# Attention scores as two full-height products of stacked queries, with two more key transfers a batch

## The chip, the cores and the metric

The kernel runs on one core of a Trainium2 chip. The metric is the device time of one execution in microseconds, the median of three runs. A core has TensorE (PE, with its weight loads PEld), VectorE (DVE), ScalarE (ACT), GpSimd (POOL) and SyncE (SP), which here only issues transfers.

## The reference

A cross-attention block and a mixture of experts over 16 batches of 256 tokens of width 256, in float32:

```
h = layernorm(x);  q = (h @ Wq + bq) as 16 heads of 16
k, v = (ctx @ Wkv + bkv) as 16 heads of 16, 77 context rows
scores = einsum('bqhd,bkhd->bhqk', q, k) / 4
x = x + (softmax(scores) @ v) @ Wp + bp
x = x + sum over the 2 best of 8 experts of gate * expert(layernorm(layernorm(x)))
```

## The kernel before

The first 300 us or so are the attention. Its 4096 tokens are 32 row tiles of 128 tokens (NT), two for each batch b of 16. A round i works on several tiles at once: it forms the scores of tile i, transposes and multiplies the probabilities of tile i-1, projects tile i-2, makes the new residual row (`x1`) of tile i-2, and prepares the queries and values of batch nb = i // 2 + 1, which rounds 2 nb and 2 nb + 1 will use. An even round is the first of a batch. Each engine runs one program in its own written order; semaphores hold them together. After round 31 the expert tiles follow; the change leaves their instructions as they are.

**Scores.** The 16 heads are two chunks (m = 0, 1) of 128 query channels, and a chunk is two halves (g = 0, 1) of 64 channels, four heads each. The keys of four heads stand as blocks on a diagonal of `k_blocks` (4 x 77 = 308 columns), so that one product of 64 channels gives the 308 scores of four heads. For float32 accuracy query and key are each split into a high and a low float32r part, and three products are summed: high query x high key, low query x high key, high query x low key. Both halves of one chunk are written as alternating products, each on its own 64 of the 128 rows of TensorE and into its own PSUM bank (L1727 to L1743). There are three score banks in turn, u = 4 i + 2 m + g; the six products of a chunk wait once, for the bank of the second half.

**Queries.** In an odd round ACT writes `q_t` (L927) and rounds it to `q_h` (L932, one operation on 128 partitions), and DVE subtracts to `q_l` (L1279, one operation).

**Keys.** `k_parts` holds high and low keys of two batches. SP's queue spreads them over the diagonal with eight transfers a batch, one for each head of a chunk (`spread_keys`, L517), in an even round, behind the store of `x1` (L539) that waits for DVE. In the odd round it issues a load of x (L498), every second time one of the context (L503), and two loads of values (`load_values`, L531 and L534), then the next store of `x1`.

**DVE.** `softmax_input` takes the maxima of both halves (L1238) and subtracts them (L1244), which frees the score banks.

Of the kernel before, what the change touches and what calls it, by code (L numbers as in the profile page):

```python
# [8 lines left out]
F32 = mybir.dt.float32  # L9
F32R = mybir.dt.float32r  # L10
# [3 lines left out]
ACTF = mybir.ActivationFunctionType  # L14
AXX = mybir.AxisListType.X

P = 128
BATCH, SEQ, D = 16, 256, 256
CTX = 77
# [235 lines left out]
def build(nc, a, out):  # L255
    with ExitStack() as ctx:
# [8 lines left out]
        def sems(name, n):  # L265
            return [sem(f"{name}{i}") for i in range(n)]
# [7 lines left out]
        f_x, f_ctx = sems("f_x", XR), sems("f_ctx", 2)  # L274
        f_kblocks, f_vstore, f_vload = (sems(n, 2) for n in ("f_kblocks", "f_vstore", "f_vload"))
        f_x1, f_put = sems("f_x1_", 3), sems("f_put", ZR)
# [84 lines left out]
        xl[0] = sb("xl0", [P, DC, WIDTH], F32R)  # L361
        wh[0] = sb("wh0", [P, 3, 2, HIDDEN], F32R)
        wl[0] = sb("wl0", [P, 3, 2, HIDDEN], F32R)

# [8 lines left out]
        v_rep = [sb(f"v_rep{i}", [P, KB, VW]) for i in range(2)]  # L373
        k_blocks = [sb(f"k_blocks{i}", [P, 2, DC, HPB, CTX], F32R) for i in range(2)]
        q_h = [sb(f"q_h{i}", [P, DC, SEQ], F32R) for i in range(2)]
        q_l = [sb(f"q_l{i}", [P, DC, SEQ], F32R) for i in range(2)]
        v_blocks = [sb(f"v_blocks{i}", [P, KB, BLOCK_HEADS, VW]) for i in range(2)]
# [115 lines left out]
        def sync_program(e):  # L493
# [14 lines left out]
            def spread_keys(b):  # L508

                e.wait_ge(k_low, b // 2 + 1)  # L510
                if b == 0:
                    e.wait_ge(blocks_ready, 2)
                if b >= 2:
                    e.wait_ge(scores_mm, SCORES_OF_BATCH * (b - 1))
                for h in range(HPC):
                    part = slice(h * HD, (h + 1) * HD)
                    e.dma_start(k_blocks[b % 2][part, :, :, h % HPB, :].bitcast(F32),  # L517
                                k_parts[part, :, :, b % 2, :].bitcast(F32)).then_inc(
                                    f_kblocks[b % 2], 16)

            def store_values(b):
# [116 lines left out]
            for i in range(FIRST_ROUND, OVERLAP + 2):  # L638
# [11 lines left out]
                if batch and i % 2:  # L650
                    load_values(nb)
                if i == EARLY_TILES + 9:
                    load_matrix(0, 0)
                    wait_puts(EARLY_TILES // 2)
                    load_rows(0)
# [8 lines left out]
                if batch and i % 2 == 0:  # L664
                    if nb == 0:
                        spread_keys(nb)
                    store_values(nb)
                    if nb:
                        spread_keys(nb)
# [56 lines left out]
        def pool_program(e):  # L726
# [79 lines left out]
            for i in range(2):  # L806
                e.memset(k_blocks[i][:, :, :, :, :].bitcast(F32), 0.0).then_inc(blocks_ready, 1)
            e.memset(half[:, :], -0.5).then_inc(half_ready, 1)
# [83 lines left out]
        def act_program(e):  # L892
# [26 lines left out]
            def queries(b):  # L919
                ps = misc_of("q", b)  # L920
                e.wait_ge(q_mm, b + 1)
                if b:
                    e.wait_ge(q_low, b)
                else:
                    e.wait_ge(bq_ready, 1)
                for m in range(DC):
                    e.activation(q_t[:, m, :], ps[:, m * SEQ:(m + 1) * SEQ], ACTF.Identity,  # L927
                                 bias=bq_scaled[:, m:m + 1], scale=SCALE).then_inc(q_out, 1)
                e.wait_ge(q_out, 2 * b + 2)
                if b >= 2:  # L930
                    e.wait_ge(scores_mm, SCORES_OF_BATCH * (b - 1))
                e.activation(q_h[b % 2][:, :, :], q_t[:, :, :], ACTF.Copy).then_inc(q_high, 1)  # L932

# [286 lines left out]
        def dve_program(e):  # L1220
# [56 lines left out]
            def low_queries(b):  # L1277
                e.wait_ge(q_high, b + 1)
                e.tensor_tensor(q_l[b % 2][:, :, :], q_t[:, :, :],  # L1279
                                q_h[b % 2][:, :, :].bitcast(F32), ALU.subtract).then_inc(q_low, 1)  # L1280

# [436 lines left out]
        def pe_program(e):  # L1718
# [8 lines left out]
            def scores(i, m):  # L1727
                b, s = divmod(i, 2)
                if s == 0 and m == 0:
                    e.wait_ge(q_low, b + 1)  # L1730
                    e.wait_ge(f_kblocks[b % 2], 16 * HPC * (b // 2 + 1))
                u0 = 4 * i + 2 * m
                if u0 >= 2:
                    e.wait_ge(less_max, u0 - 1)
                for k, (qs, w) in enumerate(((q_h, 0), (q_l, 0), (q_h, 1))):
                    for g in range(2):
                        mm = e.matmul(  # L1737
                            score_bank[(u0 + g) % 3][:, 0:HPB * CTX],
                            qs[b % 2][g * HALF:(g + 1) * HALF, m, s * P:(s + 1) * P],
                            k_blocks[b % 2][g * HALF:(g + 1) * HALF, w, m, :, :].rearrange(  # L1740
                                "p h k -> p (h k)"), start=(k == 0), stop=(k == 2))
                        if k == 2:
                            mm.then_inc(scores_mm, 1)  # L1743

# [421 lines left out]
```

## Time and profile before

| | |
|---|---|
| median of 3 runs | 935.6 us (935.13 to 937.54) |
| the profiled execution's own time | 938.24 us |
| its span, first to last instruction | 936.4 us |
| busy share of the span: PE, PEld, DVE, ACT, POOL | 95%, 85%, 80%, 69%, 44% |
| mean granted TensorE clock | 0.989 of full speed |
| attention, about | 0 to 300 us |

The shares are means over stages with different limits, so they don't tell what a part of the attention waits for; its rows do. Times in rows are counted from the first instruction, 1.8 us of the profiled time lie outside the span.

### The profile page before, as it was taken

What the parts mean: (1) busy time and instruction counts of PE and PEld (TensorE: products, weight loads), DVE (VectorE), ACT (ScalarE), POOL (GpSimd) and SP (SyncE); (2) the same over time, 40 slices, a digit from 0 to 9 for tenths busy, and PEclk for the clock granted to TensorE, in tenths of its full rate; (3) what the DMA queues carried; (4) which work ended last, traced back from release to release, by engine and by line L of the source; (5) the groups of instructions that cost most, each with busy time, mean ns of one, the idle gap of its engine ahead of it and who ended that gap; (6) DMA issues with size and microseconds to landing.
All of it is one profiled execution on the core that took longest, in us unless ns stands there. A gap on an engine that the chain in (4) does not pass through costs nothing.

```text
span 936.4 us, 19131 instructions
## 1 busy us (share of the span) xinstructions
PE 887.6 (95%) x6174; PEld 795.6 (85%) x6174; DVE 745.0 (80%) x1757; ACT 646.3 (69%) x1297; POOL 408.9 (44%) x649
## 2 busy tenths in 40 slices
PE   4999999999998998999999999999999999999995
PEld 3888878887877876788999989899898998998994
DVE  2688888888878888787979788887877877778783
ACT  3676766767666774775977777867776776777773
POOL 3456576777776575330432240605114234052052
PEclk8899999999999999999999999999999999999998
DMA  6332333342255337643756455827817838466442
GB/s 144 66 67 49 74 85 69 86 99 61 63 128 177 114 118 268 182 112 121 217 121 185 135 155 168 240 94 186 278 45 215 282 68 259 177 178 177 147 79 27
DMA packets 132368, 129.17 MB, mean 138 GB/s; under 512 B 59936, under 2 KB 117152, under 8 KB 132128
## 3 DMA queue, kind: packets, MB, share of 16 engines
q1 hardware_dynamic: 119392, 110.36, 38.7%
q0 software_dynamic: 12864, 17.44, 10.3%
q8 instruction: 55, 0.90, 0.4%
q14 instruction: 57, 0.47, 0.2%
HBM read 102.01 MB, written 25.36 MB: 136 GB/s over the span
## 4 chain that ended last, share of the span: by engine, by line
PE 78%; DVE 11%; issue 3%; ACT 3%; another core or an unknown queue 1%; POOL 1%; SPq 1%; DMA 0%; POOLq 0%; DVEq 0%; ACTq 0%
PE bank L1985 35%; PE bank L2029 18%; PE bank L1820 5%; PE bank L1737 4%; PE bank L1977 3%; PE bank L1755 3%; PE bank L1774 2%; DVE maxes L1238 2%; PE bank L1784 2%; PE bank L2017 1%; PE bank L1954 1%; DVE probs L1244 1%; DVE q_l L1279 1%; PE bank L1792 1%
## 5 line engine op out<-in xcount | busy, mean ns | idle before, releaser
L852 POOL DMA_INDIRECT out_rows<-yo,token x68 | 114.4, 1682 | 384.9 <-ACT yo L1095 319.8
L1985 PE MATMUL bank<-xh,wh 128*128 128x512 f32 (+1 forms) x672 | 234.7, 349 | 5.4 <-DVE gate_in L1610 4.8
L1985 PE MATMUL bank<-xl,wh 128*128 128x512 f32 (+1 forms) x672 | 228.9, 341 | 0.0
L1985 PE MATMUL bank<-xh,wl 128*128 128x512 f32 (+1 forms) x672 | 228.5, 340 | 0.0
L1586 DVE TENSOR_TENSOR wl<-raw,wh 128x1024 fp32r<-128x1024 f32 x126 | 152.4, 1220 | 13.0 <-ACT wh L1026 12.1
L1985 PEld LDWEIGHTS bank<-xh,wh 128*128 128x128 f32 x672 | 127.9, 190 | 20.1 <-DVE gate_in L1610 7.5
L2029 PE MATMUL bank<-wh,hh 128*128 128x256 f32 x496 | 141.9, 286 | 1.7 <-issue 1.3
L1985 PEld LDWEIGHTS bank<-xh,wl 128*128 128x128 f32 x672 | 127.8, 190 | 14.9
L2029 PE MATMUL bank<-wh,hl 128*128 128x256 f32 x496 | 140.4, 283 | 0.0
L2029 PE MATMUL bank<-wl,hh 128*128 128x256 f32 x496 | 140.4, 283 | 0.0
L1985 PEld LDWEIGHTS bank<-xl,wh 128*128 128x128 f32 x672 | 128.2, 191 | 10.8
L1026 ACT ACTIVATE wh<-raw 128x1024 fp32r<-128x1024 f32 x126 | 131.1, 1054 | 0.0
L1630 DVE TENSOR_TENSOR hl<-gate_in,hh 128x512 fp32r<-128x512 f32 x128 | 87.9, 686 | 44.8 <-ACT hh L1089 29.7
L1089 ACT ACTIVATE hh<-gate_in 128x512 fp32r<-128x512 f32 x128 | 80.2, 626 | 31.4 <-DVE gate_in L1623 28.9
L1064 ACT ACTIVATE gate_in<-bank,par 128x512 f32<-128x512 f32 x88 | 60.2, 684 | 59.7 <-PE bank L1985 54.3
L2029 PEld LDWEIGHTS bank<-wh,hh 128*128 128x128 f32 x496 | 95.0, 192 | 5.0 <-issue 1.5
L2029 PEld LDWEIGHTS bank<-wl,hh 128*128 128x128 f32 x496 | 95.1, 192 | 2.6
L2029 PEld LDWEIGHTS bank<-wh,hl 128*128 128x128 f32 x496 | 94.9, 191 | 0.0
L1076 ACT ACTIVATE gate_in<-gate_in 128x512 f32<-128x512 f32 (+1 forms) x144 | 86.0, 598 | 0.0
L1238 DVE TENSOR_REDUCE maxes<-bank 128x4 f32<-128x308 f32 x128 | 55.1, 469 | 32.0 <-PE bank L1737 26.3
L799 POOL DMA_INDIRECT z_rows<-z,slot x64 | 69.2, 1081 | 21.2 <-issue 17.7
L1820 PE MATMUL bank<-v_blocks,probs_t 128*128 128x102 f32 (+4 forms) x640 | 76.9, 274 | 0.6 <-ACT probs_t L951 0.4
(195 smaller groups left out, 1861.6 us busy)
## 6 DMA issues: line engine op xcount, KB each, us to landing
raw<-in_W SPq DMA_DIRECT2D x42, 1024.0 KB
raw<-in_Wo SPq DMA_DIRECT2D x25, 1024.0 KB
whole<-in_W SPq DMA_DIRECT2D x8, 1024.0 KB, 7.6
xs<-in_x SPq DMA_DIRECT2D x32, 128.0 KB, 2.7
out_rows<-x SPq DMA_DIRECT2D x32, 128.0 KB, 1.8
shared<-z_rows SPq DMA_DIRECT2D x7, 520.0 KB
bo_row<-in_bo SPq DMA_DIRECT2D x25, 128.0 KB
k_blocks<-k_parts SPq DMA_DIRECT2D x128, 19.2 KB
```

The costliest lines, as they stand in the source:

```text
L799: e.indirect_dma_start(out=z_rows, out_offset=bass.IndirectOffsetOnAxis(ap=slot[:, 2 * p + t, k:k + 1], axis=0), in_=z[p % ZR][:, t, :], i ...
L852: e.indirect_dma_start(out=out, out_offset=bass.IndirectOffsetOnAxis(ap=token[j % 4][:, s:s + 1], axis=0), in_=yo[j % 2][:, s, :], in_offs ...
L1026: e.activation(wh[split_before(j) % 2][:, w, c, :], raw[w][:, c, :], ACTF.Copy).then_inc(w_high, 1)
L1064: e.activation(dst[:, :], ps[:, 0:WIDTH], ACTF.Identity, bias=par[j % PR][:, X_B2 + u:X_B2 + u + 1]).then_inc(gate_out, 1)
L1076: e.activation(gate_in[n % 3][:, 0:w], gate_in[n % 3][:, 0:w], ACTF.Silu).then_inc(silu_made, 1)
L1089: e.activation(dst, hid[n % 3][:, 0:w], ACTF.Copy).then_inc(hid_high, 1)
L1238: e.tensor_reduce(maxes[i % 2][:, hs], view, AXX, ALU.max).then_inc(max_found, 1)
L1586: e.tensor_tensor(wl[q][:, w, c, :], raw[w][:, c, :], wh[q][:, w, c, :].bitcast(F32), ALU.subtract).then_inc(w_low, 1)
L1630: e.tensor_tensor(hl[n % (HR - 1)][:, :], hid[n % 3][:, :], hh[n % HR][:, :].bitcast(F32), ALU.subtract).then_inc(hid_low, 1)
L1820: mm = e.matmul(out, probs_t[i % 2][0:size, k, :], moving, start=(k == 0), stop=(k == KB - 1), skip_group_check=True)
L1985: mm = e.matmul(ps[:, h * cols:(h + 1) * cols], ws[split_before(j) % 2][:, w, c, m * P:(m + 1) * P], xx[j % 2][:, c, 0:cols], start=(h == ...
L2029: mm = e.matmul(down_bank[s // 2][:, (s % 2) * D:(s % 2 + 1) * D], hs[:, at:at + P], ws[q][:, 2, m // 4, (m % 4) * D:(m % 4 + 1) * D], sta ...
```

## The change

- The queries of half g are stacked: `q_parts[:, m, g, :]` has the high part on the 64 partitions of that half and the low part on the other 64. ACT rounds each half by itself and DVE subtracts each half by itself, writing to the other partitions.
- `k_blocks` gets a place for each half of all 128 partitions. With w = 0 the high keys stand on their own 64 partitions and, copied, on the other 64; with w = 1 the low keys stand on their own and zeros (from a memset) on the others. One product of 128 rows with w = 0 gives high x high plus low x high; one with w = 1 gives high x low. So a half takes two products of 128 rows, and a chunk four.
- The copy is `double_keys`: SP waits until the eight transfers of the batch have landed and issues two more, each 64 partitions x 2 x 308 float32 (154 KB). For batch 0 it stands right behind them, ahead of the store of values; for the others behind `load_values` in the odd round. PE waits for them (`f_kdouble`).
- The halves follow each other on PE. The first waits for its own bank only, which was freed a chunk earlier; the second has the wait that all six had.
- The blocks of even batches lie in the memory of weights that are loaded after the attention; the memsets at the start are twice as large.

```diff
@@ sync_program
                 for h in range(HPC):
+                    g, j = divmod(h, HPB)
                     part = slice(h * HD, (h + 1) * HD)
-                    e.dma_start(k_blocks[b % 2][part, :, :, h % HPB, :].bitcast(F32),
+                    e.dma_start(k_blocks[b % 2][part, :, :, g, j, :].bitcast(F32),
...
+            def double_keys(b):
+
+                e.wait_ge(f_kblocks[b % 2], 16 * HPC * (b // 2 + 1))
+                for g in range(2):
+                    own, other = (slice(r * HALF, (r + 1) * HALF) for r in (g, 1 - g))
+                    e.dma_start(k_blocks[b % 2][other, 0, :, g, :, :].bitcast(F32),
+                                k_blocks[b % 2][own, 0, :, g, :, :].bitcast(F32)).then_inc(
+                                    f_kdouble[b % 2], 16)
...
                 if batch and i % 2:
                     load_values(nb)
+                    if nb:
+                        double_keys(nb)
...
                     if nb == 0:
                         spread_keys(nb)
+                        double_keys(nb)
                     store_values(nb)
@@ pool_program
-                e.memset(k_blocks[i][:, :, :, :, :].bitcast(F32), 0.0).then_inc(blocks_ready, 1)
+                e.memset(k_blocks[i][:, :, :, :, :, :].bitcast(F32), 0.0).then_inc(blocks_ready, 1)
@@ act_program, queries
-                e.activation(q_h[b % 2][:, :, :], q_t[:, :, :], ACTF.Copy).then_inc(q_high, 1)
+                for g in range(2):
+                    part = slice(g * HALF, (g + 1) * HALF)
+                    e.activation(q_parts[b % 2][part, :, g, :], q_t[part, :, :],
+                                 ACTF.Copy).then_inc(q_high, 1)
@@ dve_program, low_queries
-                e.wait_ge(q_high, b + 1)
-                e.tensor_tensor(q_l[b % 2][:, :, :], q_t[:, :, :],
-                                q_h[b % 2][:, :, :].bitcast(F32), ALU.subtract).then_inc(q_low, 1)
+                for g in range(2):
+                    part = slice(g * HALF, (g + 1) * HALF)
+                    other = slice((1 - g) * HALF, (2 - g) * HALF)
+                    e.wait_ge(q_high, 2 * b + g + 1)
+                    e.tensor_tensor(q_parts[b % 2][other, :, g, :], q_t[part, :, :],
+                                    q_parts[b % 2][part, :, g, :].bitcast(F32),
+                                    ALU.subtract).then_inc(q_low, 1)
@@ pe_program, scores
                 if s == 0 and m == 0:
-                    e.wait_ge(q_low, b + 1)
                     e.wait_ge(f_kblocks[b % 2], 16 * HPC * (b // 2 + 1))
+                    e.wait_ge(f_kdouble[b % 2], 32 * (b // 2 + 1))
                 u0 = 4 * i + 2 * m
-                if u0 >= 2:
-                    e.wait_ge(less_max, u0 - 1)
-                for k, (qs, w) in enumerate(((q_h, 0), (q_l, 0), (q_h, 1))):
-                    for g in range(2):
-                        mm = e.matmul(
-                            score_bank[(u0 + g) % 3][:, 0:HPB * CTX],
-                            qs[b % 2][g * HALF:(g + 1) * HALF, m, s * P:(s + 1) * P],
-                            k_blocks[b % 2][g * HALF:(g + 1) * HALF, w, m, :, :].rearrange(
-                                "p h k -> p (h k)"), start=(k == 0), stop=(k == 2))
-                        if k == 2:
-                            mm.then_inc(scores_mm, 1)
+                for g in range(2):
+                    if s == 0 and m == 0:
+                        e.wait_ge(q_low, 2 * b + g + 1)
+                    if u0 + g >= 3:
+                        e.wait_ge(less_max, u0 + g - 2)
+                    for k in range(2):
+                        mm = e.matmul(score_bank[(u0 + g) % 3][:, 0:HPB * CTX],
+                                      q_parts[b % 2][:, m, g, s * P:(s + 1) * P],
+                                      k_blocks[b % 2][:, k, m, g, :, :].rearrange(
+                                          "p h k -> p (h k)"),
+                                      start=(k == 0), stop=(k == 1))
+                    mm.then_inc(scores_mm, 1)
```

On SP's queue these rows stand around the values of batch 3, before the change:

```order
L539 DMA out_rows<-x_2 128x256
L523 DMA v_flat<-v_sb 77x16x17
L517 DMA k_blocks<-k_parts 16x4x77 x8
L498 DMA xs<-in_x 128x256
L503 DMA raw<-in_ctx 128x308
L531 DMA v_rep<-v_flat 128x9x17
L534 DMA v_rep<-v_flat 80x17
L539 DMA out_rows<-x_0 128x256
```

The same place of the changed kernel, where the numbers of lines are its own:

```order
L554 DMA out_rows<-x_2 128x256
L538 DMA v_flat<-v_sb 77x16x17
L523 DMA k_blocks<-k_parts 16x4x77 x8
L503 DMA xs<-in_x 128x256
L508 DMA raw<-in_ctx 128x308
L546 DMA v_rep<-v_flat 128x9x17
L549 DMA v_rep<-v_flat 80x17
L532 DMA k_blocks<-k_blocks 64x2x308 x2
L554 DMA out_rows<-x_0 128x256
```

Only the two copies are new; they are the last transfers ahead of the scores that need them. On PE a round's start, from the transposes of a later tile to the second chunk of scores, reads before:

```order
L1792 MATMUL bank<-const,xn 128x128 x2
L1755 MATMUL bank<-const,probs 128x128 x4
L1763 MATMUL bank<-const,attn 128x128 x2
L1755 MATMUL bank<-const,probs 128x128 x4
L1841 MATMUL bank<-raw,shared 128x154 x4
L1853 MATMUL bank<-shared,raw 77x256 x2
L1737 MATMUL bank<-k_blocks,q_h 128x308 x2
L1737 MATMUL bank<-k_blocks,q_l 128x308 x2
```

and in the changed kernel:

```order
L1818 MATMUL bank<-const,xn 128x128 x2
L1781 MATMUL bank<-const,probs 128x128 x4
L1789 MATMUL bank<-const,attn 128x128 x2
L1781 MATMUL bank<-const,probs 128x128 x4
L1867 MATMUL bank<-raw,shared 128x154 x4
L1879 MATMUL bank<-shared,raw 77x256 x2
L1764 MATMUL bank<-k_blocks,q_parts 128x308 x4
L1781 MATMUL bank<-const,probs 128x128
```

Nothing moves past anything else; four products stand where six stood.

## Rows read from the trace of the kernel before

**Rows 1.** Windows: us, then busy us (instructions) of PE, PEld, DVE, ACT, POOL, clock, DMA.

```profile
50.00:115.00 65.00, 64.39 (x492) 55.26 (x491) 53.80 (x180) 46.53 (x120) 38.40 (x81) 1.00 0.29 59
150.00:186.00 36.00, 34.18 (x262) 29.14 (x262) 29.99 (x107) 24.81 (x67) 26.24 (x49) 1.00 0.37 83
```

**Rows 2.** Waits of PE from 115 to 262 us: total, times, longest.

```profile
PE bank L1737 <- DVE probs L1244: 5.3, 6, 1.3
```

**Rows 3.** Timeline of PE, first scores of batch 8: start, us, instruction, form, count.

```profile
152.75 1.05 PE L1820 MATMUL bank<-v_blocks,probs_t 128*128 128x102 f32 x8
153.74 0.41 PE L1737 MATMUL bank<-k_blocks,q_h 64*128 64x308 f32 x2
153.99 0.30 PE L1737 MATMUL bank<-k_blocks,q_l 64*128 64x308 f32 x2
...
154.36 0.44 PE L1792 MATMUL bank<-const,xn 128*128 128x128 f32 x2
```

**Rows 4.** Timeline of PE in the experts: full-height float32r products of 256 columns.

```profile
520.00 0.28 PE L1985 MATMUL bank<-xh,wh 128*128 128x256 f32 x1
520.12 0.28 PE L1985 MATMUL bank<-xl,wh 128*128 128x256 f32 x1
```

**Rows 5.** The tile q_h: count, ns min/median/max, first and last start, form.

```profile
L932 ACT ACTIVATE q_h<-q_t x16: 629/630/631, 16.4 to 278.2; 128x512 fp32r<-128x512 f32 x16
L1279 DVE TENSOR_TENSOR q_l<-q_t,q_h x16: 654/962/1251, 17.0 to 282.2; 128x512 fp32r<-128x512 f32 x16
```

**Rows 6.** Timeline of DVE in round 15: its wait ahead of x1.

```profile
153.70 0.42 DVE L1274 TENSOR_TENSOR x<-bank,xs 128x256 f32<-128x256 f32 x1 [1.13 <-remote]
```

**Rows 7.** Timeline of SP's queue, batch 3: the last value load, the next store.

```profile
64.20 0.60 SPq L534 DMA_DIRECT2D v_rep<-v_flat  x1
64.88 0.40 SPq L539 DMA_DIRECT2D out_rows<-x  x1
```

**Rows 8.** DMA issues from 0 to 300 us: count, KB each, median us from issue to landing.

```profile
out_rows<-x SPq DMA_DIRECT2D x29, 128.0 KB, 1.8
...
raw<-in_ctx SPq DMA_DIRECT2D x8, 154.0 KB, 2.7
```

**Rows 9.** Timeline of SP's queue, the last value load of batch 2.

```profile
47.83 0.62 SPq L534 DMA_DIRECT2D v_rep<-v_flat  x1
```

**Rows 10.** Timeline of PE, first scores of batch 2.

```profile
49.81 0.41 PE L1737 MATMUL bank<-k_blocks,q_h 64*128 64x308 f32 x2
```

**Rows 11.** Timeline of PE, first scores of batch 3.

```profile
65.55 0.41 PE L1737 MATMUL bank<-k_blocks,q_h 64*128 64x308 f32 x2
```

**Rows 12.** Timeline of SP's queue, the last value load of batch 9.

```profile
170.44 0.57 SPq L534 DMA_DIRECT2D v_rep<-v_flat  x1
```

**Rows 13.** Timeline of PE, first scores of batch 9 and second chunk of that round.

```profile
171.72 0.41 PE L1737 MATMUL bank<-k_blocks,q_h 64*128 64x308 f32 x2
...
176.83 0.40 PE L1737 MATMUL bank<-k_blocks,q_h 64*128 64x308 f32 x2 [0.56 <-DVE probs L1244]
```

**Rows 14.** Timeline of SP's queue, the last value load of batch 8.

```profile
151.10 0.62 SPq L534 DMA_DIRECT2D v_rep<-v_flat  x1
```

**Rows 15.** Timeline of SP's queue at the start: keys of batch 0, then its values' store.

```profile
13.09 5.27 SPq L517 DMA_DIRECT2D k_blocks<-k_parts  x8
18.41 0.59 SPq L523 DMA_DIRECT2D v_flat<-v_sb  x1
...
31.43 0.60 SPq L534 DMA_DIRECT2D v_rep<-v_flat  x1
```

**Rows 16.** Timeline of PE at the start: first scores of batch 0 and of batch 1.

```profile
19.80 0.63 PE L1737 MATMUL bank<-k_blocks,q_h 64*128 64x308 f32 x2 [4.36 <-DMA k_blocks<-k_parts]
...
33.92 0.41 PE L1737 MATMUL bank<-k_blocks,q_h 64*128 64x308 f32 x2
```

**Rows 17.** Timeline of POOL at the start: the memsets, and a wait for values.

```profile
0.73 2.19 POOL L807 MEMSET k_blocks<- 128x1232 f32 x2 [0.29 <-POOLq L2155]
...
25.88 1.77 POOL L787 TENSOR_TENSOR v_blocks<-v_rep,const 128x153 f32<-128x153 f32 x6 [10.17 <-DMA v_rep<-v_flat]
```

More of the change, by code:

```diff
@@ L274, in build @@
         f_x, f_ctx = sems("f_x", XR), sems("f_ctx", 2)
-        f_kblocks, f_vstore, f_vload = (sems(n, 2) for n in ("f_kblocks", "f_vstore", "f_vload"))
+        f_kblocks, f_kdouble, f_vstore, f_vload = (
+            sems(n, 2) for n in ("f_kblocks", "f_kdouble", "f_vstore", "f_vload"))
         f_x1, f_put = sems("f_x1_", 3), sems("f_put", ZR)
@@ L361, in build @@
         xl[0] = sb("xl0", [P, DC, WIDTH], F32R)
-        wh[0] = sb("wh0", [P, 3, 2, HIDDEN], F32R)
-        wl[0] = sb("wl0", [P, 3, 2, HIDDEN], F32R)
+        first_parts = sb("first_parts", [P, 3, 2, 2, HIDDEN], F32R)
+        wh[0], wl[0] = first_parts[:, :, 0, :, :], first_parts[:, :, 1, :, :]
         scope.append(ExitStack())
@@ L373, in build @@
         v_rep = [sb(f"v_rep{i}", [P, KB, VW]) for i in range(2)]
-        k_blocks = [sb(f"k_blocks{i}", [P, 2, DC, HPB, CTX], F32R) for i in range(2)]
-        q_h = [sb(f"q_h{i}", [P, DC, SEQ], F32R) for i in range(2)]
-        q_l = [sb(f"q_l{i}", [P, DC, SEQ], F32R) for i in range(2)]
+        k_blocks = [first_parts[:, 2, :, :, :].rearrange("p w c n -> p (w c n)")[
+            :, 0:4 * DC * HPB * CTX].rearrange("p (w m g h k) -> p w m g h k", w=2, m=DC, g=2, h=HPB),
+                    sb("k_blocks1", [P, 2, DC, 2, HPB, CTX], F32R)]
+        q_parts = [sb(f"q_parts{i}", [P, DC, 2, SEQ], F32R) for i in range(2)]
         v_blocks = [sb(f"v_blocks{i}", [P, KB, BLOCK_HEADS, VW]) for i in range(2)]
@@ L510, in spread_keys @@
                 e.wait_ge(k_low, b // 2 + 1)
-                if b == 0:
-                    e.wait_ge(blocks_ready, 2)
+                if b < 2:
+                    e.wait_ge(blocks_ready, b + 1)
                 if b >= 2:
@@ L922, in queries @@
                 if b:
-                    e.wait_ge(q_low, b)
+                    e.wait_ge(q_low, 2 * b)
                 else:
```

## The prediction

> **What bounds the kernel now.** I read the windows first, to see which engine is full in which stretch of the attention; then PE's waits, to see where it isn't the bound; then the timelines of PE, SP's queue and DVE around the first scores of a batch, since the change adds a wait there; then the sizes and landings of transfers.
>
> In the windows [rows 1] PE is busy 64.39 of 65.00 us between 50 and 115 us: that stretch is PE's alone, and DVE has 11 us to spare. From 150 to 186 us PE has 34.18 of 36.00, so 1.8 us of idle in two batches. The waits say whose that is: from 115 to 262 us PE waits 5.3 us in 6 waits, 0.9 us each, for DVE's subtraction ahead of scores [rows 2]. So up to round 11 every us on PE counts, and later PE and DVE hand the path to each other: PE from the second chunk of an even round through the odd round's scores, then DVE, which has maxima, queries, x1 and softmax to do before the second chunk of the next even round.
>
> **What the change takes away.** *Products.* The two halves of a pair already run at once: two instructions take 0.41 us together, and the next pair starts 0.25 us behind [rows 3]. Six products fill 0.62 us (153.74 to 154.36). Ahead of them is a gap: eight value products starting at 152.75 fill 1.05 us, so the last, at 0.28 us, starts at about 153.53, and 0.21 us pass until 153.74, where value products follow each other every 0.11 us. A chunk thus costs 154.36 - 153.53 = 0.83 us. After the change it is 0.11, then four full-height products. Those of 256 columns start 0.12 us apart [rows 4], so 308 columns take 308 / 256 x 0.12 = 0.14: 0.11 + 4 x 0.14 = 0.67. **0.16 us saved a chunk**, I take 0.15; for 64 chunks 9.6 us of PE's work, of which only what lies on the path counts.
>
> The Trainium skill has a rule on this (TensorEngine Tiling, Key Properties): a change of tiling mode drains TensorE, while different tiles can work in parallel. The rows show both, the gaps of 0.21 and 0.25 us and the simultaneous pair. By its second half alone, four slots of 0.14 us in place of three would cost 0.14 us a chunk, and 9 us in all.
>
> *The wait of the second chunk.* Where PE waits for DVE, it does two products afterwards and not six: 0.62 - 0.28 = 0.34 us less. DVE gets the first half's scores about 0.2 us earlier, since they end before the other half's begin. With the chunk in between, the PE part of a late batch gets 0.34 + 0.15 + 0.2 = 0.7 us shorter.
>
> **What it adds.** *ACT and DVE.* Each half has as many elements a partition as the whole had: ACT +0.63 us, DVE +0.65 to +1.25 us (its median 0.96) a batch [rows 5]. That 64 partitions take as long as 128 no row shows; the bounds are nothing (if they took half) and one more whole operation, and I take a whole. ACT hides it: it is busy 46.53 of 65 us [rows 1]. Up to 115 us DVE's is hidden in its idle time. Later it is on the path, less what fits into DVE's wait ahead of x1, 1.13 us in the round shown [rows 6]. That wait doesn't stand in every round, so I take +0.4 us of 0.96. A late batch thus changes by -0.7 + 0.4 = **-0.3 us**, if nothing else holds it.
>
> *The landing of the copies.* This term decides. PE's first scores of a batch need them, everything on PE stands behind that wait, and SP issues them only after `load_values`. Let L be the time from the end of that issue to the landing of the second copy. The first copy's issue takes 0.4 to 0.6 us, as other transfers there [rows 7]. Then a landing: no row shows a copy inside the chip of this size. The nearest are stores of 128 KB, 1.8 us, and loads of just 154 KB, 2.7 us [rows 8]. So L lies between 0.4 + 1.8 = 2.2 and 0.6 + 2.7 = 3.3; the values' packets stand ahead in the same queues, so I take the middle, **L = 2.8**.
>
> The Trainium skill (DMA: Bandwidth & Descriptors, Anatomy of one DMA) fits 2.0 us plus bytes at 436 GB/s to one transfer of GpSimd's path, which is 2.4 us for 154 KB; taken over to SP's it makes L 2.9 by this estimate and the sum under 1 us higher. No row separates its two parts.
>
> Against L stands the slack S, from the end of the values' issue to the first scores before the change:
> - batch 2: 47.83 + 0.62 = 48.45, scores at 49.81 [rows 9, 10]: S = 1.36
> - batch 3: 64.80, scores at 65.55 [rows 7, 11]: 0.75
> - batch 8: 151.72, scores at 153.74 [rows 3, 14]: 2.02
> - batch 9: 171.01, scores at 171.72 [rows 12, 13]: 0.71
>
> Odd batches have less, since SP loads a context for them. The stall is L - S. Off it come the 0.3 us that PE saves between two stores of x1, by which SP's loop is timed, and PE's idle time later in the round, where it waits for DVE anyway (0.56 us in batch 9 [rows 13], 0.9 on average [rows 2]). Batch 2: 1.44 - 0.3 = 1.1. Batch 3: 2.05 - 0.3 = 1.75. Batch 9: 2.09 - 0.3 - 0.56 = 1.2. Batch 8: 0.78 - 0.3 - 0.9, so nothing. From the same two timelines for each of the fourteen batches 2 to 15: 2 to 5 pay 1.1, 1.75, 0.1, 0.3 = **+3.3**; 7, 9 and 11 pay 1.2, 1.2, 0.7 = **+3.1**; the other seven pay nothing and keep their 0.3: **-2.1**.
>
> *The start.* For batch 0 nothing hides it. SP's issue of keys ends at 18.36 and PE starts at 19.80 [rows 15, 16], so the keys have landed at about 19.7. The copies are issued until 20.8. The store of values, issued at 18.41 [rows 15], goes out 2.4 us later, and POOL, which waits 10.17 us until 25.88 for these values [rows 17] and makes statistics of later tiles behind them, is 2.4 us later too. Batch 1 adds its own L - S: 31.43 + 0.60 = 32.03, scores at 33.92, S = 1.9 [rows 15, 16], 0.9 - 0.3 = 0.6. The memset of 2.19 us doubles [rows 17]; what waits for it moves by nothing to 2.2 us, and as the first loads land 2.7 us after their issue and later [rows 8] I take 0.2. Together 2.4 + 0.6 + 0.2 = **+3.2**.
>
> **Sum.** 3.2 + 3.3 + 3.1 - 2.1 = +7.5 us. The profiled execution took 938.24, so 945.7 for one like it; that one lies 2.6 us above the median of 935.6, and with the same difference the median becomes 943.1: **I say 943 us**. The experts take their usual time. PE's clock was full in both windows [rows 1]; I add no term for it.
>
> **The rivals.**
> 1. *The stall is hidden and PE's saving counts: faster.* It decides if L is at most about 1.7, less than the nearest landing plus an issue. For it speak that a copy inside the chip touches no HBM, and that key transfers of 19 KB land 1.4 us after the end of their issue [rows 15, 16]. Then the start costs 2.4 + 0.2, batch 3 pays 0.65, all others together bring 2.8, and with DVE's extra hidden (0.4 in ten late batches) the sum is -3.5 us: 932. Chance 0.16.
> 2. *It balances, within 0.3% of before.* L = 2.2: the start costs 2.6, batches 2, 3, 7, 9, 11 pay 0.5, 1.15, 0.6, 0.6, 0.1, batches 4 and 5 gain 0.5 together, the other seven 2.1: +3.0, and +0.2 with DVE's extra hidden in seven batches. 936 to 938. Chance 0.20.
> 3. *DVE becomes the bound as well.* Subtractions of 1.25 us, the second not hidden: +0.9 in place of +0.4 in ten late batches, 5 us on top of the forecast: 948. With L = 3.3, 0.5 more in eight batches, 952. Chance 0.12.
> 4. *The forecast*, stalls of 1 to 2 us behind the copies in the start and in six or seven batches: 0.52, its own range 939 to 948.
>
> A measurement of this kernel tells 0.3% or 2.8 us from no change. Slower is above 938.4: the forecast and rival 3, 0.64. Within it 0.20, faster 0.16. The range takes rival 1's time in part and leaves out the ends of rivals 1 and 3: 933 to 951.
>
> **What the profile would show.** Scores as one row of four products, some 0.6 us, and the next instruction 0.67 us behind the last one before. A wait of PE for the copies at the first scores of batches 0 to 3, 7, 9 and 11, and about none in 12 to 15; its end less the end of the values' issue is L. DVE's q_parts as 32 operations of 0.65 to 1.25 us. First scores of batch 1 near 37 us in place of 33.92. The prediction is wrong if the copies land within 1.7 us, if an operation on 64 partitions takes half, if full-height products of 308 columns take over 0.18 us (the saving is then a loss), or if late batches wait for something that the trace before doesn't show.

## The result and the profile after

The changed kernel takes 979.37 us (median of 4, 976.71 to 982.33), the kernel before, run beside it, 936.57: ratio 1.0445 [1.0386, 1.0503], 42.8 us slower. The forecast was 943, range 933 to 951: right in direction, far off in size. The profiled execution took 982.33 us with a mean clock of 0.961, where that of before had 0.989.

The same two stretches as in [rows 1], in the changed kernel:

```profile
50.00:115.00 65.00, 56.73 (x407) 53.64 (x406) 49.98 (x156) 43.28 (x107) 32.86 (x73) 0.97 0.37 75
150.00:186.00 36.00, 31.15 (x212) 29.54 (x213) 27.54 (x96) 22.47 (x57) 22.46 (x43) 0.91 0.38 89
```

PE idles 8.3 of 65 and 4.9 of 36 us, where it idled 0.6 and 1.8, and the granted clock, 1.00 before, is 0.97 and 0.91. Both are new. PE's waits from 50 to 300 us:

```profile
PE bank L1764 <- issue: 30.8, 12, 4.0
PE bank L1810 <- ACT q_t L945: 0.5, 1, 0.5
```

L1764 is the scores' product. Twelve times, once a batch, it stands still 2.6 us on average, and the releaser reads "issue": this view names nobody. The waits for DVE of [rows 2] are gone; its work now fits behind the stall. Around the first scores of batch 8, SP's queue (start, us, instruction, count) and PE:

```profile
163.82 0.34 SPq L554 DMA_DIRECT2D out_rows<-x  x1
164.20 0.39 SPq L538 DMA_DIRECT2D v_flat<-v_sb  x1
164.68 5.64 SPq L523 DMA_DIRECT2D first_parts<-k_parts  x8
...
171.49 0.60 SPq L549 DMA_DIRECT2D v_rep<-v_flat  x1
172.13 1.32 SPq L532 DMA_DIRECT2D first_parts<-first_parts  x2
174.46 0.35 SPq L554 DMA_DIRECT2D out_rows<-x  x1
```

```profile
172.74 1.17 PE L1846 MATMUL bank<-v_blocks,probs_t 128*128 128x68 f32 x9
176.59 1.23 PE L1764 MATMUL bank<-first_parts,q_parts 128*128 128x308 f32 x4 [2.69 <-issue]
177.62 0.63 PE L1818 MATMUL bank<-const,xn 128*128 128x128 f32 x2
...
180.39 1.03 PE L1879 MATMUL bank<-shared,raw 128*77 128x256 f32 x4
181.07 0.91 PE L1764 MATMUL bank<-first_parts,q_parts 128*128 128x308 f32 x4
```

The x1 store, the values' store, eight keys, x, two value loads and two copies stand in one line on SP, and PE starts 3.1 us behind the last copy's issue. The view of the transfers issued from 172.8 to 173.5 us has the second copy and its time to landing:

```profile
first_parts<-first_parts SPq DMA_DIRECT2D x1, 154.0 KB, 3.7
```

Issued at 172.8, it lands at 176.5, and the scores start at 176.59: PE waits for the copies, though the view of waits does not say so. The end of the values' loads to the first scores is 176.59 - 172.09 = 4.50 us here, the L of the prediction; over batches 2 to 15 it is 3.50 to 5.35. All sixteen batches have the stall ahead of their first scores, 43.5 us together, against 6.3 before.

After the stall the four products take 1.23 us instead of some 0.8, and two transposes 0.63 instead of 0.38. The windows of these stretches give the clock:

```profile
176.80:180.10 3.30, 3.30 (x16) 3.27 (x16) 2.55 (x9) 1.77 (x5) 1.95 (x4) 0.50 0.03 8
180.30:184.00 3.70, 3.70 (x29) 3.27 (x28) 2.50 (x8) 3.34 (x9) 1.45 (x2) 1.00 0.00 0
```

PE is fully busy in both, at 1.2 GHz in the first and 2.4 GHz in the second. From 19 us to the end of the attention the mean clock is 0.91 over 324 us, thus some 58 us at half, against 0.98 over 283 us, some 11, before.

From timelines of both kernels, the fourteen batches 2 to 15, in us, each from the first scores of a batch to those of the next:

| | before | after | after less before |
|---|---|---|---|
| first scores to the next x1 store on SP | 103.0 | 110.3 | +7.3 |
| x1 store to the end of the values' loads | 118.9 | 119.0 | +0.1 |
| from there to the next batch's first scores | 27.1 | 57.1 | +30.0 |
| sum | 249.0 | 286.3 | +37.4 |

The start adds 4.9: the first scores of batch 1 come at 38.85 and not at 33.92 [rows 16]. Together that is the 42.3 us by which batch 15 begins later.

### The profile page after: what moved, and what is told of

It reads as the page before. It is cut to its first block, busy times and chain, and to the rows that moved or that the text cites. A ratio compares the mean times of both kernels' runs of the same rounds, so it can differ in the third digit from the quotient of the medians.

```text
span 980.5 us, 18970 instructions
## 1 busy us (share of the span) xinstructions
PE 901.4 (92%) x6046; PEld 832.8 (85%) x6046; DVE 758.7 (77%) x1773; ACT 657.8 (67%) x1313; POOL 416.6 (42%) x649
## 4 chain that ended last, share of the span: by engine, by line
PE 84%; issue 6%; ACT 3%; POOL 2%; DVE 2%; SPq 2%; DMA 1%; POOLq 0%; DVEq 0%; ACTq 0%
PE bank L2011 35%; PE bank L2055 18%; PE bank L1846 6%; PE bank L1764 4%; PE bank L1781 4%; PE bank L2003 3%; PE bank L1810 3%; PE bank L1800 2%; PE bank L2043 2%; PE bank L1980 1%; PE bank L1867 1%; PE bank L1879 1%; SPq L523 1%; PE bank L1789 1%; PE bank L1856 1%
## 5 line engine op out<-in xcount | busy, mean ns | idle before, releaser
L2011 PE MATMUL bank<-xh,first_parts 128*128 128x256 f32 (+1 forms) x704 | 153.9, 305 | 0.5 <-DVE probs L1265 0.4
L2011 PE MATMUL bank<-xh,wh 128*128 128x512 f32 (+1 forms) x320 | 127.0, 397 | 1.4 <-DVE gate_in L1635 1.2
L2011 PE MATMUL bank<-xl,wh 128*128 128x512 f32 (+1 forms) x320 | 122.6, 383 | 0.0
L2011 PE MATMUL bank<-xh,wl 128*128 128x512 f32 (+1 forms) x320 | 122.1, 382 | 0.0
L2011 PEld LDWEIGHTS bank<-xh,first_parts 128*128 128x128 f32 x704 | 116.4, 191 | 6.0 <-DVE gate_in L1635 0.8
L2011 PE MATMUL bank<-xl,first_parts 128*128 128x256 f32 (+1 forms) x352 | 106.5, 303 | 0.0
L1611 DVE TENSOR_TENSOR first_parts<-raw,first_parts 128x1024 fp32r<-128x1024 f32 x66 | 79.9, 1222 | 3.1 <-ACT first_parts L1047 2.4
L1611 DVE TENSOR_TENSOR wl<-raw,wh 128x1024 fp32r<-128x1024 f32 x60 | 72.9, 1221 | 10.3 <-ACT wh L1047 10.0
L1846 PEld LDWEIGHTS bank<-v_blocks,probs_t 128*128 128x128 f32 (+1 forms) x640 | 75.8, 192 | 2.5 <-ACT probs_t L972 1.6
L2055 PE MATMUL bank<-first_parts,hh 128*128 128x256 f32 x384 | 73.7, 289 | 1.2 <-issue 1.2
```

What stands on the lines that cost most here:

```text
L1611: e.tensor_tensor(wl[q][:, w, c, :], raw[w][:, c, :], wh[q][:, w, c, :].bitcast(F32), ALU.subtract).then_inc(w_low, 1)
L1846: mm = e.matmul(out, probs_t[i % 2][0:size, k, :], moving, start=(k == 0), stop=(k == KB - 1), skip_group_check=True)
L2011: mm = e.matmul(ps[:, h * cols:(h + 1) * cols], ws[split_before(j) % 2][:, w, c, m * P:(m + 1) * P], xx[j % 2][:, c, 0:cols], start=(h == ...
L2055: mm = e.matmul(down_bank[s // 2][:, (s % 2) * D:(s % 2 + 1) * D], hs[:, at:at + P], ws[q][:, 2, m // 4, (m % 4) * D:(m % 4 + 1) * D], sta ...
```

## The experiments

Theory A: PE stands still behind the copies, and the clock that falls after each stall costs on top. Rival B: the divided operations, or the full-height products, cost the time. Rival C: the copies as traffic, or as work of SP, do. Ratios are against the kernel before on the same chip.

**No copies.** `double_keys` isn't called and PE's wait for it is gone.

```diff
                     load_values(nb)
-                    if nb:
-                        double_keys(nb)
...
-                    e.wait_ge(f_kdouble[b % 2], 32 * (b // 2 + 1))
```

> The changed kernel without the two copies of each batch and without TensorE's wait for them; the products and their shapes stay. It leaves out the product of low queries with high keys (the other partitions of the high key blocks stay zero). Theory A (TensorE standing still behind the copies makes the loss, and the clock that falls to half after it adds to it): the sixteen stalls go from 43.5 us back to about 5, the granted clock of 50 to 300 us goes back to 1.00, and what remains is the saving of 0.10 to 0.15 us a chunk: 930 us, between 924 and 936. Rival B (the two 64-partition operations each on ScalarE and VectorE, or the full-height products, cost the time): 955 us or more. Rival C (the copies as traffic and as work of the SP queue, not TensorE's wait): about 930 here too, told apart by the next kernel.

Measured: 933.77 us, ratio 0.9960 [0.9932, 0.9989]. The stalls ahead of the batches' first scores are 5.1 us, the clock from 50 to 300 us is full, and the scores follow the values at once:

```profile
152.66 0.50 PE L1842 MATMUL bank<-v_blocks,probs_t 128*128 128x68 f32 x3
152.96 0.81 PE L1760 MATMUL bank<-first_parts,q_parts 128*128 128x308 f32 x4
153.61 0.38 PE L1814 MATMUL bank<-const,xn 128*128 128x128 f32 x2
```

The last value product, at 0.28 us, starts at 152.66 + 0.50 - 0.28 = 152.88, so a chunk is 153.61 - 152.88 = 0.73 us, where before it was 0.83. The second chunk of an odd round, which has another product ahead of it, goes from 0.93 us (166.93 to 167.85 before) to 0.78 (166.47 to 167.26 here). Rival B falls: with all its operations and products in place the kernel is 3.6 us faster than before.

**Dead copies.** The copies are issued as in the changed kernel, into buffers that nothing reads.

```diff
-                    e.dma_start(k_blocks[b % 2][other, 0, :, g, :, :].bitcast(F32),
+                    e.dma_start(spare[b % 2][other, :, 0:HPB * CTX].bitcast(F32).rearrange(
+                                    "p m (h k) -> p m h k", h=HPB),
...
-                    e.wait_ge(f_kdouble[b % 2], 32 * (b // 2 + 1))
```

> The changed kernel with its copies issued in the same places and of the same bytes, but into two buffers that nothing reads, and TensorE does not wait for them. It leaves out the product of low queries with high keys. Theory A: as without copies, 930 to 938 us; the copies' issue of 1.3 us on SP in the odd round delays SP's later stores by that, which nothing waits for. Rival C (traffic or SP's queue is the cost): near 979, at least 960. Rival B: 955 or more.

Measured: 938.93 us, ratio 1.0011 [0.9984, 1.0037]. 5.2 us over the kernel without copies, and 3.3 of these are the start (batch 1 begins at 38.11 and not at 34.82), where the copies' issue goes ahead of the values' store. From the first scores of batch 1 to those of batch 15 the two traces agree, 244.3 us without copies and 244.1 with dead ones. So C is worth 5 us, and not 40.

**Before, with the wait.** The products and queries of before, plus the two copies into idle buffers, and PE waits for them.

```diff
                     load_values(nb)
+                    if nb:
+                        double_keys(nb)
...
                     e.wait_ge(f_kblocks[b % 2], 16 * HPC * (b // 2 + 1))
+                    e.wait_ge(f_kdouble[b % 2], 32 * (b // 2 + 1))
```

> The kernel before, with its six half-height products a chunk and whole-tile queries, plus the same two copies a batch into buffers that nothing reads, and with TensorE waiting for them before the first scores of each batch. Nothing is left out. Theory A: the wait alone makes the loss, and without the saving of the stacked products: 981 to 990 us, stalls of 2 to 4 us at all sixteen batches and the same falls of the clock. Rival B: 945 us or less, since the operations that it blames are absent.

Measured: 984.95 us, ratio 1.0490 [1.0448, 1.0532]. The copies and the wait for them make the whole loss, 47.6 us, without any of the change's products and queries; the copies without the wait cost 5 in the run before this one. And this trace, where the copies write buffers of their own, names what "issue" hid. PE's waits from 50 to 300 us, and the window of 50 to 115:

```profile
PE bank L1756 <- DMA xl<-k_blocks: 16.5, 6, 3.9
PE bank L1756 <- DMA xh<-k_blocks: 14.3, 6, 3.1
```

```profile
50.00:115.00 65.00, 58.64 (x410) 50.57 (x407) 43.50 (x135) 39.26 (x97) 29.52 (x64) 0.92 0.30 61
```

Twelve waits and 30.8 us, as many and as much as the "issue" of the changed kernel. The clock of this window is 0.92.

**Busy through the stall.** Fillers ahead of the wait, in the changed kernel.

```diff
+                    if b >= 2:
+                        e.wait_ge(less_max, u0 - 2)
+                        stay_busy(40, score_bank[u0 % 3])
                     e.wait_ge(f_kblocks[b % 2], 16 * HPC * (b // 2 + 1))
```

> The changed kernel with 40 filler products of 128 columns ahead of the first wait of each batch from batch 2 on, so that TensorE works through about 2.2 us of each stall; nothing else. Theory A, split in two: the stalls stay (33 to 40 us of them, part now shown as filler), but the clock stays full in batches 2 to 15. In the changed kernel 58 us of the stretch 19 to 344 us lie at half clock against 11 before, and TensorE's busy time is 10 us more in spite of 7 to 9 us of products saved, so that the clock part is some 17 us: 960 us, between 955 and 968. If the clock were no part of it (stall alone): 977 to 984, or more where a stall is shorter than the fillers.

Measured: 965.96 us, ratio 1.0288 [1.0246, 1.0329], 13.4 us under the changed kernel (14.7 by the ratios). Around batch 8:

```profile
170.81 0.67 PE L1912 MATMUL bank<-ones 128*128 128x128 bf16 x9
172.78 0.80 PE L1767 MATMUL bank<-first_parts,q_parts 128*128 128x308 f32 x4 [1.30 <-issue]
173.42 0.38 PE L1821 MATMUL bank<-const,xn 128*128 128x128 f32 x2
```

```profile
150.00:186.00 36.00, 33.66 (x288) 31.69 (x285) 29.02 (x102) 23.02 (x62) 23.64 (x45) 1.00 0.36 83
```

The copies still land late, but from batch 2 on PE idles at most 1.5 us ahead of first scores, and the clock from 50 to 300 us stays full. In the split of the table: 91.2, 119.3 and 59.5, sum 269.9. The way from the loads to the scores is no shorter than in the changed kernel (57.1), the way from the scores to the x1 store is 19.1 us shorter. So the loss has two parts, and this run separates them: about 30 us of late copies, and on PE's own work the clock, 13 us at least (the fillers can also cost where a stall was shorter than they; that way is 2.4 us longer here).

**Copies ahead of the values' loads.**

```diff
-                    load_values(nb)
                     if nb:
                         double_keys(nb)
+                    load_values(nb)
```

> The changed kernel with the two copies ahead of the values' loads in the odd round, and the keys where they were. Nothing is left out. It asks what the copies wait for. In batch 8 the last key transfer is issued by 170.32, the values' loads by 172.09, the copies at 172.13. If the copies stood in SP's line alone, they start 1.1 us earlier, and the stalls of batches 1 to 15 shrink by about 1.1 us each, with their share of the clock: 955 to 968 us. If the keys' landing (about 2 us behind the last issue) holds them, they start at 172.1 to 172.4 as now, and the values' loads come 2.4 us later: 976 to 990 us.

Measured: 965.15 us, ratio 1.0286 [1.0225, 1.0347]. SP's queue of one odd round, its first row the last five keys:

```profile
157.59 3.16 SPq L523 DMA_DIRECT2D first_parts<-k_parts  x5
160.80 0.59 SPq L503 DMA_DIRECT2D xs<-in_x  x1
162.18 1.31 SPq L532 DMA_DIRECT2D first_parts<-first_parts  x2
163.59 0.54 SPq L546 DMA_DIRECT2D v_rep<-v_flat  x1
```

SP stands still 0.8 us ahead of the copies, until the keys have landed, 1.4 us behind the end of their issue (160.75). The rest of the way to the copies was the line on SP, as expected: the stalls are 34.1 us, where they were 43.5.

**Keys first.** In the even round the keys go ahead of the x1 store, in the odd one the copies ahead of the loads; and, as a control, the keys' move alone in the kernel before.

```diff
+                if nb and batch and i % 2 == 0:
+                    spread_keys(nb)
                 if 0 <= i - 2 < NT:
                     store_x1(i - 2)
...
                     store_values(nb)
-                    if nb:
-                        spread_keys(nb)
```

> The changed kernel with its transfers in another order on SP, from batch 1 on: the eight key transfers go first in the even round, ahead of the store of x1 (which waits for the end of that round) and of the values' store, and the two copies go ahead of the values' loads in the odd round. Nothing is left out. Theory A, now with a reason for the period: in the changed kernel x1's store, the values' store, the keys, the values' loads and the copies stand in one line on SP, 12.8 us from the x1 store at 163.82 to the scores at 176.59, and the next x1 store comes 7.4 us after these, so that a batch takes 20.2 us where 17.7 us would do. With the keys out of that line the copies should be issued some 10 us after the scores of the batch before and land 3 us later, ahead of need in every batch but the first: 935 us, between 930 and 943, stalls of 5 to 10 us in all, a full clock from 60 us on. Rival D (the latency of a copy that follows other transfers, 3.5 to 5.4 us, is there wherever it stands): 960 us or more.

> The kernel before with the key transfers first in the even round, ahead of x1's store, as a control for the reordered kernel: theory A expects no difference, 935 to 939 us, as nothing waited for the keys there. A gain of more than 3 us would say that part of what the reordered kernel wins is not the copies'.

Measured: 960.61 us, 1.0224 [1.0181, 1.0268]; and the control 968.12 us, 1.0296 [1.0248, 1.0345]. Both expectations missed: the move itself costs 29 us. SP, DVE and POOL in the control:

```profile
159.51 5.07 SPq L517 DMA_DIRECT2D k_blocks<-k_parts  x8
164.63 0.58 SPq L539 DMA_DIRECT2D out_rows<-x  x1
165.25 0.38 SPq L523 DMA_DIRECT2D v_flat<-v_sb  x1
...
171.27 0.60 SPq L534 DMA_DIRECT2D v_rep<-v_flat  x1
```

```profile
156.05 0.42 DVE L1332 TENSOR_TENSOR v_sb<-bank,rows 77x256 f32<-77x256 f32 x1
...
159.01 0.47 DVE L1250 TENSOR_TENSOR k_parts<-raw,k_parts 128x308 fp32r<-128x308 f32 x1
```

```profile
173.55 1.77 POOL L787 TENSOR_TENSOR v_blocks<-v_rep,const 128x153 f32<-128x153 f32 x6 [4.04 <-DMA v_rep<-v_flat]
```

Every second batch SP waits for `k_parts`, which DVE makes at 159.48; the values, ready at 156.47, are stored at 165.25, and POOL gets them late. From the late values the chain goes over POOL's `v_blocks` and ACT's y and logits to PE. From 50 to 300 us PE waits for it, where it didn't in the kernel before:

```profile
PE bank L1871 <- ACT logits L974: 10.8, 5, 2.3
```

Yet the reordered kernel with the copies is 7.5 us faster than this control, and no run shows why; part may be the stacked products, part the clock, 0.94 from 50 to 300 us against 0.92 in the control. Of its batches 2 to 15 seven have no stall ahead of their first scores, seven one of 1.9 to 3.8 us.

**Copies on ScalarE.** Two operations in the odd round in place of the two transfers, and PE waits for them.

```diff
+            def double_blocks(b):
+                e.wait_ge(f_kblocks[b % 2], 16 * HPC * (b // 2 + 1))
+                for g in range(2):
+                    own, other = (slice(r * HALF, (r + 1) * HALF) for r in (g, 1 - g))
+                    e.activation(
+                        k_blocks[b % 2][other, 0, :, g, :, :].rearrange("p m h k -> p m (h k)"),
+                        k_blocks[b % 2][own, 0, :, g, :, :].bitcast(F32).rearrange(
+                            "p m h k -> p m (h k)"), ACTF.Copy).then_inc(k_doubled, 1)
...
                     probs_t_copy(i - 1, 2)
+                if batch and not even:
+                    double_blocks(nb)
```

> The changed kernel with the high key blocks copied to the other partitions by two ScalarE operations of 64 partitions in the odd round, in place of the two transfers; SP's order is the changed kernel's. Nothing is left out. Theory A: some 1.5 us more on ScalarE a batch, which has room, and the copy ends 1.5 to 2 us after the keys have landed, at about the time of the scores: stalls under 1 us in most batches, 936 us, between 931 and 946. Rival D': the keys land too late for any copy behind them; stalls of 1.5 us or more in most batches and 955 us or more.

Measured: 937.39 us, ratio 0.9975 [0.9949, 1.0000]: the loss is gone. ACT and PE ahead of the first scores of batch 8:

```profile
153.65 0.60 ACT L1018 ACTIVATE y<-x,shift,scale 128x256 f32<-128x256 f32 x1
...
154.59 1.46 ACT L957 ACTIVATE first_parts<-first_parts 64x616 fp32r<-64x616 f32 x2
```

```profile
156.15 0.81 PE L1773 MATMUL bank<-first_parts,q_parts 128*128 128x308 f32 x4 [0.47 <-issue]
```

A gap of 0.43 to 0.48 us stands ahead of the first scores of nearly every batch. I tried its two readings.

**One wait less.** PE waits for `k_doubled` alone.

```diff
-                    e.wait_ge(f_kblocks[b % 2], 16 * HPC * (b // 2 + 1))
                     e.wait_ge(k_doubled, 2 * b + 2)
```

> The kernel with ScalarE's copies, in which TensorE no longer waits for the key transfers themselves ahead of a batch's first scores, only for ScalarE's copies, which were made behind them. Nothing is left out. With both waits TensorE idles 0.43 to 0.48 us (in one batch 0.86) before these scores in batches 2 to 15 although all that it waits for is over, and its gap is put down to issue; without copies it is 0.00. Theory F (this gap is the price of one more wait in TensorE's stream): the gap goes, 14 times 0.47 = 6.6 us, 931 us, between 927 and 936. Rival: the gap is the end of ScalarE's copy, and stays: 936 to 939 us.

Measured: 936.77 us, ratio 0.9989 [0.9959, 1.0019]. Theory F falls; the gap stays, and now the trace names its cause:

```profile
156.52 0.83 PE L1772 MATMUL bank<-first_parts,q_parts 128*128 128x308 f32 x4 [0.43 <-ACT first_parts L957]
```

**ScalarE's y behind the copies.**

```diff
-                if 0 <= i - 3 < NT:
+                if not (batch and not even) and 0 <= i - 3 < NT:
                     make_y(i - 3)
...
                 if batch and not even:
                     double_blocks(nb)
+                    if 0 <= i - 3 < NT:
+                        make_y(i - 3)
```

> The kernel with ScalarE's copies and one wait, in which ScalarE takes its scaling of y (0.60 us, L1018) behind the copies in the odd rounds, instead of ahead of them. Nothing is left out. In both kernels with ScalarE's copies these begin 0.02 us behind another ScalarE operation and end 0.10 us (0.04 with one wait) ahead of the first scores, in every batch from 2 on: ScalarE's place in line, not the number of waits, is what TensorE's 0.43 us hang on. Theory G: the copies end up to 0.6 us earlier, the gap goes to 0.0 to 0.1 us in batches 2 to 15, 14 times 0.4 = 6 us: 931 us, between 927 and 936. Rival: the keys land no earlier than ScalarE takes them now (the last key transfer is issued 2.5 us before), and the gap and 937 us stay; or y's later readers on GpSimd give it back, with a gap of 0 and 935 to 939 us.

Measured: 944.66 us, ratio 1.0069 [1.0032, 1.0106]. The gap does go (0.00 to 0.35 us from batch 2 on), and the kernel is slower than either side expected. Three waits, one of POOL and two of PE, from 60 to 290 us:

```profile
POOL xf L758 <- ACT y L1018: 40.7, 23, 6.8
```

```profile
PE bank L1774 <- DVE probs L1276: 7.9, 7, 1.4
PE bank L1791 <- ACT probs L965: 4.9, 11, 0.4
```

With y ahead of the copies the first is 36.7 us in 16 waits and the second 4.6 in 6 (33.1 and 4.4 with both of PE's waits in place), and the third doesn't appear: ACT's exponentials, which PE's transposes need, are later now. The second theory of the gap's place was right, and removing it moved the wait.

**The divided query operations alone,** in the kernel before: both engines' (first), and DVE's alone (second).

```diff
-                e.activation(q_h[b % 2][:, :, :], q_t[:, :, :], ACTF.Copy).then_inc(q_high, 1)
+                for g in range(2):
+                    part = slice(g * HALF, (g + 1) * HALF)
+                    e.activation(q_h[b % 2][part, :, :], q_t[part, :, :],
+                                 ACTF.Copy).then_inc(q_high, 1)
```

> The kernel before with only the queries' two operations cut into two of 64 partitions each on ScalarE and on VectorE (both still write the buffers of before, the products wait for both). Nothing is left out. Theory A, by the prediction's own terms: one more operation of 0.63 us on ScalarE, one of 0.65 to 1.25 us on VectorE a batch, the latter met again at the first scores of the late batches, which is where 4.5 us of the expected saving went: 938 to 943 us. Rival E (the lost part of the saving lies in the products, not in the operations): 936 to 938 us, no difference.

> The kernel before with only VectorE's low queries cut into two operations of 64 partitions; ScalarE's high queries stay one operation. Nothing is left out. With both cut the kernel was 0.63% slower than before. If VectorE's 10 to 20 us of more work is the price: 943 to 946 us, as with both cut. If ScalarE's 10 us are (a later high part delays the low part and the round's exponentials): 937 to 940 us.

Measured: 945.56 us, 1.0063 [1.0037, 1.0089], and 951.65 us, 1.0140 [1.0085, 1.0196]. The first says that the division costs 6.6 us, more than the 1 to 5 expected. The operation's row shows why it can: on ACT half the partitions take the whole time, on DVE the shortest operation does (0.65 us in both) [rows 5].

```profile
L934 ACT ACTIVATE q_h<-q_t x32: 626/628/631, 17.0 to 287.0; 64x512 fp32r<-64x512 f32 x32
L1284 DVE TENSOR_TENSOR q_l<-q_t,q_h x32: 647/690/1399, 17.6 to 288.1; 64x512 fp32r<-64x512 f32 x32
```

The second missed: with less work added it is slower. Its profiled execution has two falls of the clock of 10.2 us each that the first doesn't have, so its median can't tell ACT's share from DVE's. Its two executions with a clock of 0.985 and 0.987 took 946.31 and 944.83 us, within the 942.05 to 947.83 of the eight executions of the first at 0.985 to 0.988; that would put the price on DVE, but these are two executions on another chip, where the kernel before is 3.1 us faster, so it stays open.

## Why the prediction was wrong

Its direction and the mechanism it named, PE waiting for the copies behind the values' loads, were right. Step by step:

- **"I add no term for PE's clock"** failed. Granted 1.00 in both windows before, it was 0.97 and 0.91 after. The step read the clock as a property of the stretch, but it follows the stall that the change puts there. Filling the stalls gave back 13.4 us. It is the term that was missing, and the prediction gave no reason for leaving it out but the clock of the kernel without the stall.
- **L = 2.8** was mis-sized: 3.50 to 5.35, mean 57.1 / 14 = 4.1, above the upper bound of 3.3. I had counted one issue of 0.4 to 0.6 and a landing of 1.8 to 2.7. In the same terms the first copy's issue took 0.65, and 1.6 to 1.7 in batches 9 and 13; the landing, from the start of the second copy's issue, 2.6 to 4.1 us, the middle one 2.9; and in batch 14 SP stood 0.6 us ahead of the copies, until the keys had landed. So even the shortest L, 3.50, lay above my upper bound. 1.3 us in fourteen batches are 18 us, more than twice the whole sum. The estimate from the Trainium skill (DMA: Bandwidth & Descriptors, Anatomy of one DMA), L 2.9, was short too.
- **The slack S** was read rightly: its sum over batches 2 to 15 is the 27.1 of the table, and 57.1 - 27.1 = 30.0 of the 37.4 us is L - S with the true L.
- **"The other seven pay nothing"**, and the credit of 0.3 us saved between two stores of x1, failed. All seven stall, 2.0 to 2.7 us in batches 12 to 15. A mean L of 4.1 exceeds even the largest slack, 4.03 in batch 14. That batch's own L - S is next to nothing (4.06 - 4.03), and PE stands 2.7 us all the same: SP's line times the batches now, as I read it, and PE, done sooner within the longer batch, waits at its end, so that S read before is no longer PE's slack. The way from scores to x1 store got 7.3 us longer and not 4.2 shorter, which is the clock again: at full clock, with the fillers, it is 11.8 shorter than before. In all, batches 2 to 15 were to cost 4.3 us and cost 37.4.
- **The start, +3.2**, was +4.9: 3.3 from the copies ahead of the values' store (2.4 forecast), 0.7 the wait, 0.9 in the kernel without copies (0.2 forecast).
- **The products' saving** held. A first chunk takes 0.08 + 0.65 us in the kernel without copies, where 0.11 + 0.56 was forecast: 0.10 saved and not 0.16; a second chunk of an odd round saves 0.15. That kernel is 3.6 us faster than before with the divided operations in it, whose price in the kernel before is 6.6: some 10 us for the products, if that price is the same here, which no run shows; the forecast had 9.6 of PE's work, of which only a part was to count. By the second half alone of the rule in the Trainium skill (TensorEngine Tiling, Key Properties) they would have cost 9 us; that kernel excludes it.
- **A whole operation for 64 partitions** was right on ACT, 0.63 us, and for DVE's shortest one; DVE's median is 0.69 us, under the 0.96 of the whole. **Hidden on ACT, +0.4 on DVE in ten batches** (4 us) was a little low against 6.6, whose split between the engines is open.
- The rivals "hidden" and "balances" are what the kernel gives if the copies are off PE's path (0.9975 with ACT's copies). DVE did not become the bound: it is busy 27.54 us from 150 to 186 us, where it was 29.99.

## What to carry to other kernels

A transfer that is issued behind others on a full queue, and then waited for by the engine that bounds the kernel, cost here its issue, its landing and the clock that the bounding engine loses by standing still; count the last as a term of its own wherever a change puts a stall into a stretch that was full. Two copies of 154 KB each to other partitions were cheaper as two operations on ACT, which had room (1.46 us), than as two transfers (4.1 us from the queue's last load to their use). Half the partitions was no half operation: dividing ACT's by partitions doubled its time, and DVE's took 0.69 us twice for 0.96 once.

## What the runs showed of the hardware

The granted clock can fall behind a single idle. In the kernel with DVE's queries divided, one wait of 1.58 us is followed, 1.1 us after its end, by 10.24 us at half clock, with PE full all through:

```profile
127.02 0.41 PE L1740 MATMUL bank<-k_blocks,q_h 64*128 64x308 f32 x2 [1.58 <-DVE probs L1244]
```

```profile
117.50:127.80 10.30, 8.72 (x69) 7.18 (x68) 8.98 (x29) 6.63 (x17) 8.73 (x16) 1.00 0.41 104
128.10:138.30 10.20, 10.20 (x47) 9.22 (x48) 6.11 (x23) 3.68 (x14) 6.50 (x10) 0.50 0.30 64
138.40:149.00 10.60, 9.92 (x76) 8.76 (x75) 7.48 (x28) 7.22 (x19) 5.96 (x14) 1.00 0.35 85
```

A wait of 1.65 us at 205.1 us is followed by the same, as is one of 1.54 us in the kernel with one wait less; in the kernel with both divided one of 1.63 us at 271.2 is not, nor is one of 1.53 us in the kernel with dead copies. So the length of the idle alone doesn't decide it. After the stalls of 1.7 to 4.0 us of the changed kernel the fall lasted 3.4 or 6.8 us and came in eleven of the fourteen batches 2 to 15; behind 2.6, 1.7 and 2.0 us in batches 2, 4 and 15 the clock stayed full. At half the clock PE does half its work, so such a fall costs up to half its length where PE is the bound, 5 us by this estimate, and it is probably part of why executions of one kernel differ: those of the kernel without copies run from 929.46 us at a mean clock of 0.991 to 938.21 at 0.984. Differences of 2 or 3 us between single executions here mean little.

And "issue" as a releaser doesn't mean that nothing was waited for. Twice it stood for a real wait, a landing of copies in the changed kernel and an operation of ACT in the one with two waits, and a variant with one wait, or with buffers of their own, named it; for the copies the time of their landing in the same trace does too.
